# Cross attention: the transfers that place the row maxima, issued by ScalarE on its own queue instead of by SyncE

## What is computed

```python
q = _split_heads(query @ q_w + q_b, B)      # 16 heads of 16
k = _split_heads(key @ k_w + k_b, B)
v = _split_heads(value @ v_w + v_b, B)
scores = jnp.einsum('bhqd,bhkd->bhqk', q, k) * SCALE
attn = jax.nn.softmax(scores, axis=-1)
out = jnp.einsum('bhqk,bhkd->bhqd', attn, v)
```

## Time and profile before

| | |
|---|---|
| median of 3 executions | 976.96 us (973.77 to 977.6) |
| the profiled execution's own time | 969.72 us |
| its span, first to last instruction | 967.9 us |
| granted TensorE clock, mean over the span | 0.931 of full speed |
| 476 to 665 us (cross attention): PE busy | 155.04 of 189 us |
| same stretch: VectorE, ScalarE, GpSimd busy | 123.78, 102.39, 58.75 us |
| same stretch: mean busy share of the 16 DMA engines | 0.42 |

### The profile page before, as it was taken

How to read it: one execution, slowest core, us unless ns; L and a number is a source line. 1 busy time by engine, 2 the same in 40 slices (tenths; PEclk the granted TensorE clock), 3 DMA queues, 4 the chain that set the end, 5 groups by cost and what they waited for, 6 DMA issues and landing times.

```text
span 967.9 us, 17147 instructions
## 1 busy us (share of the span) xinstructions
PE 830.9 (86%) x6187; PEld 613.1 (63%) x6187; DVE 594.5 (61%) x1431; ACT 448.5 (46%) x831; POOL 350.8 (36%) x321
## 2 busy tenths in 40 slices
PE   7899789779989888787567888888997999999894
PEld 5677556667667666565345555555875777777784
DVE  5799889466888889763444677773552333333255
ACT  5677756446656654332134565666322323232221
POOL 9422100023454447530200136444530242222584
PEclk9899999879999997898658999999998999999998
DMA  5689759898968767237535454415303212221421
GB/s 170 192 254 301 219 148 260 298 228 226 267 155 219 233 183 206 76 122 227 185 104 175 141 164 148 148 59 194 100 23 95 66 57 66 67 64 41 153 66 66
DMA packets 160722, 149.18 MB, mean 154 GB/s; under 512 B 92288, under 2 KB 129216, under 8 KB 159360
## 3 DMA queue, kind: packets, MB, share of 16 engines
q1 hardware_dynamic: 157232, 138.72, 49.7%
q0 software_dynamic: 3408, 9.38, 2.6%
HBM read 86.90 MB, written 61.03 MB: 153 GB/s over the span
## 4 chain that ended last, share of the span: by engine, by line
PE 46%; DVE 13%; ACT 12%; DMA 10%; POOL 8%; issue 5%; SPq 5%; POOLq 0%; DVEq 0%; ACTq 0%
PE ps L2720 10%; PE ps L2735 5%; PE ps L2584 3%; DVE big L1445 2%; POOL hank L344 2%; POOL kept L2867 2%; DMA queries<-q_pad 2%; PE ps L422 2%; PE ps L2209 2%; PE ps L2169 2%; PE ps L1401 2%; PE ps L2098 2%; PE ps L2025 2%; DMA t_dram<-room 2%; PE ps L1393 1%
## 5 line engine op out<-in xcount | busy, mean ns | idle before, releaser
L2720 PE MATMUL ps<-wr,xbT 128*128 x312 | 101.4, 468 | 1.8 <-ACT xbT L2756 1.8
L2148 DVE TENSOR_REDUCE cmx<-ps 128x4 f32<-128x1024 f32 x64 | 77.5, 1220 | 41.2 <-PE ps L2098 41.2
L2185 ACT ACTIVATE cross_room<-ps 128x1024 f32<-128x1024 f32 x64 | 65.5, 1024 | 61.1 <-PE ps L2111 60.5
L2809 POOL DMA_INDIRECT y_dram<-yb,dest_row x39 | 37.4, 959 | 133.2 <-DVE dest_row L2785 128.7
L1361 POOL TENSOR_TENSOR st<-st,exponent 128x20 f32<-128x20 f32 x16 | 56.5, 3532 | 63.6 <-DVE st L1336 62.0
L2720 PEld LDWEIGHTS ps<-wr,xbT 128*128 128x128 f32 x312 | 59.9, 193 | 30.5 <-issue 4.2
L549 DVE SCALAR_TENSOR_TENSOR room<-room 128x256 f32<-128x256 f32 x144 | 58.3, 478 | 11.7 <-ACT room L498 11.7
L2794 DVE TENSOR_TENSOR cross_room<-cross_room,ps 128x352 f32<-128x352 f32 x39 | 20.3, 521 | 61.2 <-PE ps L2720 61.2
L2764 ACT ACTIVATE cross_room<-ps 128x352 f32<-128x352 f32 x39 | 18.1, 464 | 74.4 <-PE ps L2720 74.4
L2800 DVE TENSOR_SCALAR yb<-ps,weight 128x256 f32<-128x256 f32 x39 | 18.9, 484 | 50.8 <-PE ps L2735 50.8
L422 PE MATMUL ps<-room,weights 128*128 128x256 f32 x192 | 46.8, 396 | 3.4 <-DMA room<-in_conv_v 2.8
(11 more groups left out here) (355 smaller groups left out, 2193.9 us busy)
## 6 DMA issues: line engine op xcount, KB each, us to landing
xs_dram<-staged SPq DMA_DIRECT2D x17, 1040.0 KB, 6.7
room<-in_gW SPq DMA_DIRECT2D x8, 1280.0 KB, 8.4
tok_dram<-room SPq DMA_DIRECT2D x8, 768.0 KB, 7.5
fir_dram<-room SPq DMA_DIRECT2D x6, 1024.0 KB, 6.9
paths<-fir_dram SPq DMA_DIRECT2D x48, 128.0 KB, 3.5
keys<-k_pad SPq DMA_DIRECT2D x28, 196.0 KB
queries<-q_pad SPq DMA_DIRECT2D x28, 196.0 KB
xb<-xs_dram SPq DMA_DIRECT2D x39, 130.0 KB, 2.4
```

The lines of the kernel that those rows point to most:

```text
L2148: V.tensor_reduce(mx[:, :, half, :, g].rearrange("p t c -> p c t"), ps[:, pair(h), :].rearrange("p c (t k) -> p c t k", t=TT), AX.X, ALU.m ...
L2185: S.activation(pT[g % 2][:, pair(h)].rearrange("p c k t -> p (c k t)"), ps[:, pair(1 - h), :].rearrange("p c n -> p (c n)"), ACT.Exp, scal ...
L2720: m = nc.tensor.matmul(ps[:, 2 * (j % 2) + half, 0:FF], xbT[j % 2][:, k, :], wr[:, bass.ds(e, 1), k, half, :].rearrange("p e n -> p (e n)" ...
```

## The change

`sp_lift` and `sp_attend` go from SP's order. `act_lift` gets their body behind its copy: ScalarE waits for its own copy to be written, and issues the two transfers on its own queue. Tiles, shapes, semaphores and PE's waits stay. In the changed file the copy is L2120, the new issues L2125, and all lines behind them have numbers smaller by 9.

```diff
@@ sp_queries
             yield
             yield
-            sp_lift(b - 1, 0)
             if 1 < b < B:
                 sp_query_in(b, 0)
@@
-        def sp_lift(b, half):
-
-            copied(sp, f"mx{half}", b)
-            g = slice(half * SLOTS // 2, (half + 1) * SLOTS // 2)
-            for c in range(HL):
-                row = c * DH + ROWS - 1
-                nc.sync.dma_start(qS[home(b)][row:row + 1, g].bitcast(F32),
-                                  lift[half][c * SLOTS // 2:(c + 1) * SLOTS // 2].bitcast(F32)).then_inc(*s.lifts_in[half].up(16))
-
-        def sp_attend(b):
-            yield
-            sp_lift(b, 1)
-            yield
@@ act_lift
             act.wait_ge(s.lifts_in[half], 32 * b)
             S.copy(lift[half][:], bank(f"mx{half}", b)[0:SLOTS, 0:T]).then_inc(*out_of(f"mx{half}", b).up())
+            copied(act, f"mx{half}", b)
+            g = slice(half * SLOTS // 2, (half + 1) * SLOTS // 2)
+            for c in range(HL):
+                row = c * DH + ROWS - 1
+                nc.scalar.dma_start(qS[home(b)][row:row + 1, g].bitcast(F32),
+                                    lift[half][c * SLOTS // 2:(c + 1) * SLOTS // 2].bitcast(F32)).then_inc(*s.lifts_in[half].up(16))
@@
-        weave([ahead(sp_queries), sp_attend, idle, idle], B, sp_before)
+        weave([ahead(sp_queries), idle, idle, idle], B, sp_before)
```

## The result

| | before | after |
|---|---|---|
| median of 4 executions each, on the same chip | 975.65 us | 984.95 us (980.3 to 991.76) |
| ratio, 95% interval | | 1.0114 [1.0068, 1.016] |
| the profiled execution's own time | 969.72 us | 980.3 us |
| its span | 967.9 us | 978.5 us |
| granted TensorE clock, mean | 0.931 | 0.922 |

A later comparison with 12 executions of the change gave 1.0065 [1.0027, 1.0104]. So the change costs 6 to 9 us. The forecast was 4.5 us gained. The median of the four, 984.95 us, lies just above its range (966 to 984 us), on the slow side; the later comparison (982.42 us against 976.33) lies within it, but is a loss as well.

What follows compares the result with a forecast made beforehand. PE, busy 86% of the span, was taken as the bound. Terms 3.5 - 0.75 + 3.3 - 0.9 + 3 x 0.2 - 1.2 gave 4.5 us gained: 976.96 - 4.5 = 972.5 us, range 966 to 984.

Steps and rivals of the forecast that it cites:

- The issue's time and the pair's, 0.59 and 1.2 us: On ScalarE, behind each maxima copy: one lift issue holds the engine 0.59 us, the two together 1.2 us.
- the cheap issue: Rival: a lift issue on ScalarE takes only 0.3 us, so 9.8 us are gained, 967.2 us; chance 0.2.
- the lengthened one: ScalarE and SP issuing at once lengthen each other's issues, on ScalarE up to 1.49 us; its rival's chance 0.2.
- 4 KB should land within 3 us: First lift, PE's wait at 490.70: ScalarE's queue is served beside SP's, so the wait goes, 3.5 us gained.
- 3.3 us gained at 526.40 and 540.10 together: Early steps: the later lift's wait goes and strips come earlier, though PE still waits for them; 3.3 us gained.
- 0.75 us lost at the first copy of half 1: Copy at 492.5 us: the issues delay xT's copy right behind, 1.2 less 0.46 us of cover, 0.75 us lost.
- Half 0, `coT` 0.7 us late: Middle steps: the issues delay the copy to `coT` on ScalarE, so PE's L2169 starts 0.7 us late.
- The 0.2 us a boundary: Middle step boundaries: earlier strips, mostly spent on ScalarE's delay, gain 0.2 us at each of the last three.
- 0.9 us lost in the weights step: Step with ScalarE's shared-weights copies, 562 to 568 us: no cover, xT's copy ends at 569.1, 0.9 us lost.
- 1.2 us lost in the last step: Last step, no queries to wait for: 0.7 us from half 0 and some 0.5 from half 1, 1.2 us lost.
- The second queue is none: Rival: lift packets still stand behind the bulk, early waits stay, only issue order changes; 977.6 us, chance 0.17.
- ScalarE becomes the bound: Rival: issues hold ScalarE longer than SP, thirteen of sixteen pairs delay PE; gain gone at 0.76 us each; chance 0.2.

Runs made afterwards that it cites:

- experiment 7: The change, with SP holding the first load of expert weights (704 KB) back until the first lift has landed; 981.57 us.
- experiment 5: The change itself measured once more, against the kernel before; 982.42 us against 976.33, ratio 1.0065.
- experiment 3: The kernel before, SP issuing everything, with only the query strips moved ahead of the lift of half 0; 968.14 us, ratio 0.997.
- experiment 8: The kernel before, SP issuing everything: half-0 strips ahead of the lift, first half-1 strips and weights behind the lifts; 966.56 us, ratio 0.9882.
- experiment 9: The change, with half-0 strips first and SP issuing the bulk only after the lift, issued by ScalarE, has landed; 976.48 us, ratio 0.9986 to before.
- experiment 10: The change, with ScalarE's casts of the shared weights spread over slots 2 and 5 of the fourth step; 977.47 us, ratio 1.0019 to before.
- experiment 12: The change, with the lifts of the last batch issued by SP as before, the others by ScalarE; 979.85 us, ratio 1.0076 to before.
- experiment 6: The kernel before, with ScalarE also issuing an extra pair from `lift` to DRAM scratch behind each copy; 979.72 us, ratio 1.0021.

## Why the prediction was wrong, point by point

- **The issue's time and the pair's, 0.59 and 1.2 us: right.** 0.58 (28 of 32 within 580 and 602 ns, three of the other four at 580 to 586) and 1.19, with 1.3 us until ScalarE's next instruction starts. Neither the cheap issue nor the lengthened one came. The rule of the Trainium skill (Perfetto Trace Analysis, "DMA Instruction — HWDGE (DVE, Sync)") has sequencers, there those of DVE and Sync, lock one descriptor generator in turn; the lengthening that the prediction drew from it for ScalarE and SP isn't seen in the nine issues of the change that overlapped SP's.
- **"4 KB should land within 3 us", 3.5 us gained at 490.70: the step that failed first.** The lift issued at 487.92 was used at 494.94, 7.0 us later; the gain is 0.2 us. The DMA view of the changed kernel, packets by queue, from 488 to 493 us and from 493 to 495:

```profile
q1 hardware_dynamic: 490, 1.06, 76.9%
```

```profile
q1 hardware_dynamic: 232, 0.31, 43.2%
q10 hardware_dynamic: 16, 0.01, 1.4%
```

  ScalarE's queue moves its first 16 packets 5 us after the issue, and SP's moved 490 in the meantime. A pair issued at 497.07, with nothing else under way, moved its packets from 498.3 to 499.1. The rule that queues take turns packet by packet (the Trainium skill, DMA: Bandwidth & Descriptors, "Queues, rings and completion order") was read as keeping the whole gain; the measurement decides, and turns of that kind aren't seen in these 5 us. What decides can be counted from the same trace, as the bytes that SP had issued and its queue hadn't yet moved. At 487.92 these were 1.4 MB, and 0.3 MB when the lift's first packet moved; at 520.90 they were 1.8 MB, and 0.5 MB at its first packet, 5.7 us later. Of the change's sixteen pairs the eight that found under 0.1 MB moved their first packet 1.2 us after the issue, though SP issued 0.4 MB more beside four of them. So a transfer on the second queue waits until most of what the first one had been given before it is through. Why the chip serves it so isn't shown. The estimate had also overlooked what a freed SP does: it puts 704 KB of weights ahead of the lift, so that 1.4 MB stand there instead of the 0.7 MB of before, at a price of 1.5 us (experiment 7).
- **3.3 us gained at 526.40 and 540.10 together: right in size, but not for the reason given.** The wait for the lift is gone and the strips are late next: PE was 5.01 us later than in the trace of before at the start of the step, 518.83, and 1.74 us later at 541.84 (540.10 before), which is 3.3 gained. But this lift's queue wasn't served beside the other either. Counted from the start of the step it was issued 0.7 us earlier than before (520.90, less the 5.01, against 516.63), and its last packet moved 6.3 us after the issue (527.2), where on SP's queue, behind 2.0 MB, PE had it after 9.7 (9.3 and 10.6 in the other two traces of before). That is late, and still 3 us sooner than behind the bulk on the same queue. Experiment 2, with half 1 alone on ScalarE, has the wait gone too, and experiment 1, with half 1 on SP, has 3.9 us of it.
- **0.75 us lost at the first copy of half 1: right** (0.76: from 495.66 to 498.94 PE took 3.28 us where it had been 2.52), with PE waiting for xT at 498.94 and again at 522.77 (0.69 and 0.76 us).
- **Half 0, `coT` 0.7 us late: right in size** (mostly 0.73, six to eight times in an execution), and the middle steps that ran at the full clock (21.4 to 21.8 us) lie among those of before (21.3 to 22.0). The 0.2 us a boundary that was to be gained isn't seen. What was left out is the clock: one middle step of experiment 5 lasted 24.0 us at a clock of 0.93, with waits of 0.53, 0.32 and 1.53 us for ScalarE ahead of the lower level. Such steps are in most traces with issues on ScalarE, in none of the three of before, but also in experiments 3 and 8, where SP issues; how much of it is due to the change is open.
- **0.9 us lost in the weights step: the second step that failed**, by a term that was put at nothing, the clock. ScalarE's delay itself came out nearly as forecast, though by another path: not at xT's copy, as 0.7 of half 0 and 1.2 of half 1, but sooner, at the maxima's copy, for which PE already waited before (0.55 us at 566.21), and by half 0 alone. From the turn of the half-0 maxima to the product behind that copy PE took 11.06 us in the three traces of before and 11.86 in the two of the change, 0.8 lost. (The 1.67 us of the wait are mostly not this loss; experiment 3 has 1.49 of them.) But the whole step, from that turn to the next, took 26.02 and 24.44 us against 22.15, which is 3.1 lost in the mean: the other 2.3 are products at the lower clock (in the first trace from 571.03 to 577.64, with no wait among them). All four traces with both halves on ScalarE and SP's order of the change show this; experiments 1 and 9 have the same 0.8 us of delay (22.95 and 22.99 us in all) at the full clock. So the waits alone don't bring the lower clock, and what does is open. The table's 3.6 us for column 4 count the step from the half-1 turn, and hold some 0.5 us that were a wait for strips at the end of column 3 before. Moving the casts away gave back some 0.46%, by two series whose intervals overlap (experiment 10).
- **1.2 us lost in the last step: perhaps too low.** Against three traces of before, columns 7 and 8 lose 2.8 us together; against the first alone the step lost 4.1. Experiment 12, with the last lifts back on SP, won nothing, so that ScalarE's issues in this step are the cause isn't shown.
- **The sum.** With 0.2 in place of 3.5, 3.6 in place of 0.9, 2.8 in place of 1.2, and the middle boundaries at nothing: 0.2 - 0.75 + 3.3 - 3.6 - 2.8 = -3.65 us. The table's 3.7 is made up a little otherwise (4.6 gained in columns 2 and 3, 0.6 and 1.2 lost in columns 1 and 6), and that the two agree is in part luck. Both are under the 6 to 9 us of the medians; the rest is not accounted for. It could be executions with more steps at the lower clock, which two traces don't settle.
- **The rivals.** "The second queue is none" had the mechanism of the first wait, the packets standing behind the bulk, but not the second wait, which went. "ScalarE becomes the bound" had the right side and the wrong condition: it wanted issues of over 0.76 us. At 0.58 the losses already outweigh the gain, because the gain was half of what was counted (3.5 us of 7.4) and the lower clock came on top of the delay.

## What to carry to other kernels

An issue holds the engine that makes it (0.58 us in this form), and delays whatever stands behind it on that engine; don't give it to the engine directly ahead of the bound, even if SP seems crowded. A small urgent transfer is late by the bulk that was issued ahead of it, here on either queue: reorder the bulk behind it on the queue that has the time (here 1.2% faster, with no instruction moved to another engine). Price a delay as more than its own length only with traces at hand: here the same delay was followed by the lower clock in four traces and not in two. And take more than one trace of each kernel before a wait of 2 us is put down to a change.

## What the runs showed of the hardware that was not expected

- A transfer of 4 KB on a second, otherwise empty queue moved no packet for 5 us while the first queue had 1.4 MB ahead; with nothing ahead it was done within 1 us of its issue's end. With 1.8 MB ahead it was through 6.3 us after its issue, against 9.7 us with 2.0 MB ahead on the first queue itself.
- The time of an issue depends on its form: from `lift` to SBUF 580 ns, from the same tile to DRAM 284 ns (experiment 6), on the same engine.
- The first issue on ScalarE's queue took 1.18 us in every trace in which it was a lift, the others 0.58; to DRAM (experiment 6) it was 0.51 us.
- The same kernel, executed again, had a wait of 2.49 us at a place where it had 0.57 in the first trace.
